# Macaron transformer on one core: GpSimd instead of SyncE writes the score terms of the later batches in the first and the last attention

## What is computed

```python
x = x + 0.5 * _L0_ffn_ref(_layernorm(x, axis=-1), ...)
x = x + _L0_attn_ref(_layernorm(x, axis=-1), ...)
x = x + 0.5 * _L0_ffn_ref(_layernorm(x, axis=-1), ...)
...
x = x + 0.5 * _L3_ffn_ref(_layernorm(x, axis=-1), ...)
x = x + _L3_attn_ref(_layernorm(x, axis=-1), ...)
x = x + 0.5 * _L3_ffn_ref(_layernorm(x, axis=-1), ...)
```

```python
qkv = (x @ qkv_w.T + qkv_b).reshape(B, T, 3, H, D)
att = jnp.einsum('bhtd,bhsd->bhts', q, k) / np.sqrt(D)
att = att + bias[None]                       # layer 0 only, and causal
att = jax.nn.softmax(att, axis=-1)
out = jnp.einsum('bhts,bhsd->bhtd', att, v)
```

## Time and profile before

| | us |
|---|---|
| median of 3 runs | 1535.95 |
| lowest and highest run | 1530.17, 1540.0 |
| the profiled execution | 1542.29 |
| its span in the trace | 1540.6 |
| first attention in the trace | about 118 to 345 |
| last attention in the trace | about 1184 to 1430 |

### The profile page before, as it was taken

The page is one execution under the profiler, slowest core; times in us unless marked ns, Lnnn a source line. Parts: engine busy times, 40 slices in busy tenths (PEclk is TensorE's granted clock), DMA queues, the critical chain, the costliest instruction groups (busy, mean ns, idle before and its releaser), DMA issues. The chain is left out here.

```text
span 1540.6 us, 30124 instructions
## 1 busy us (share of the span) xinstructions
PE 1210.5 (79%) x11545; PEld 694.1 (45%) x11553; DVE 876.5 (57%) x2261; ACT 637.1 (41%) x1318; POOL 530.9 (34%) x616
## 2 busy tenths in 40 slices
PE   3995578896978748998997976683896798898498
PEld 2663244443665524555553542432574122333277
DVE  5047467742145447778644548695137888894205
ACT  1322355551322125665562224241234376776043
POOL 5753022112320067888420001126472121212442
PEclk9997799997979968999897988685897599999699
DMA  6522422103710027665416400001433212210344
GB/s 132 154 86 82 100 78 74 51 11 84 229 57 2 0 82 203 193 183 164 145 48 75 64 7 0 0 9 47 126 112 110 72 39 68 79 30 17 85 121 121
DMA packets 147513, 128.65 MB, mean 84 GB/s; under 512 B 19101, under 2 KB 133161, under 8 KB 147376
## 3 DMA queue, kind: packets, MB, share of 16 engines
q1 hardware_dynamic: 138432, 114.08, 27.6%
q0 software_dynamic: 6304, 11.37, 2.3%
q10 hardware_dynamic: 2640, 1.36, 0.6%
HBM read 79.80 MB, written 47.69 MB: 83 GB/s over the span
## 5 line engine op out<-in xcount | busy, mean ns | idle before, releaser
L2470 DVE TENSOR_REDUCE att_maxima<-psum 128x2 f32<-128x1024 f32 (+3 forms) x384 | 355.0, 949 | 133.0 <-PE psum L2118 58.0
L2351 ACT ACTIVATE att_probs<-psum 128x512 f32<-128x512 f32 (+1 forms) x640 | 323.0, 556 | 210.5 <-PE psum L2114 86.6
L108 POOL TENSOR_TENSOR rstd<-var_eps,neg_half 128x4 f32<-128x4 f32 x44 | 45.1, 1025 | 469.4 <-DVE var_eps L99 469.4
L2097 PE MATMUL psum<-att_queries,att_keys 50*32 50x384 bf16 (+4 forms) x1280 | 156.9, 331 | 47.6 <-DMA att_queries<-att_max_t 18.5
L2103 PE MATMUL psum<-att_keys,att_queries 48*32 48x384 bf16 (+4 forms) x1280 | 154.3, 343 | 12.2 <-DVE att_maxima L2470 11.8
L1045 POOL DMA_INDIRECT returned<-moe_out,moe_slot_tokens x101 | 101.3, 1003 | 123.7 <-DVE moe_out L973 97.5
L839 ACT ACTIVATE moe_hidden<-psum,moe_b 128x320 f32<-128x320 f32 (+1 forms) x128 | 77.7, 607 | 130.3 <-PE psum L752 129.7
L2097 PEld LDWEIGHTS psum<-att_queries,att_keys 50*32 50x32 bf16 (+1 forms) x1280 | 45.8, 92 | 171.6 <-issue 91.7
L172 PE MATMUL psum<-ident,normalised_rows 128*128 128x128 f32 x192 | 43.0, 365 | 96.0 <-DVE normalised_rows L117 73.0
L759 PE MATMUL psum<-moe_w,moe_hidden 128*128 128x128 f32 (+1 forms) x784 | 109.5, 286 | 0.0
L752 PE MATMUL psum<-moe_slot_columns,moe_w 128*128 128x320 f32 (+1 forms) x256 | 101.0, 539 | 2.9 <-ACT moe_slot_columns L834 2.9
(11 more groups left out here) (296 smaller groups left out, 2339.8 us busy)
## 6 DMA issues: line engine op xcount, KB each, us to landing
score_terms<-att_parts SPq DMA_DIRECT2D x44, 384.0 KB, 2.7
moe_w<-l_w SPq DMA_DIRECT2D x64, 256.0 KB, 3.1
moe_back<-returned SPq DMA_DIRECT2D x24, 256.0 KB, 4.2
att_queries<-score_terms SPq DMA_DIRECT2D x64, 96.0 KB
att_keys<-score_terms SPq DMA_DIRECT2D x64, 96.0 KB
att_queries<-score_terms SPq DMA_DIRECT2D x16, 384.0 KB, 4.3
att_keys<-score_terms SPq DMA_DIRECT2D x16, 384.0 KB, 5.3
dispatched<-untaken SPq DMA_DIRECT2D x2, 2064.0 KB, 25.8
```

What stands on the lines that cost most here:

```text
L2097: col = nc.tensor.matmul(g.psum[one, cols_bank + h, c0:c0 + w], k_op[own_rows, ci, p, key], q_op[own_rows, ci, p, first_query[s]:T], start ...
L2351: nc.scalar.activation(probs[:, G % 2, 2 * p + r, unit_at[u]:unit_at[u] + w], g.psum[:, cols_bank + r, 0:w], ACT.Exp).then_inc(probs_ready, 1)
L2470: ins = nc.vector.tensor_reduce(maxima[:, G % 2, t, 2 * p:2 * p + 2], g.psum[:, rows_bank(k):rows_bank(k) + 2, c0:c0 + w], axis=AX, op=ALU ...
```

## The change

In the first and last attention (`split`), the writes of the terms of batches 1 to 3 are issued by GpSimd and no longer by SyncE. `write_terms(b, side)` stands right behind `low_parts(b, side)` in GpSimd's list, so side 0 is written in slot 4b-6 and side 1 in slot 4b-5 (batch 1: slots -2 and -1, where SyncE issued it in slot 0). SyncE keeps the writes of batch 0, the loads and the maxima. As two engines now issue writes, batch 0's other rows count on a semaphore of their own (`other_written`), and `await_written` picks the one to wait on. Sizes, shapes and number of transfers stay as they are.

```diff
-    def write_side(self, sp, b, side, rows, done):
+    def write_side(self, queue, b, side, rows, done):
...
-            sp.dma_start(dst[at:at + n, rows, :].rearrange("j r t -> r j t"), src).then_inc(done, 16)
+            queue.dma_start(dst[at:at + n, rows, :].rearrange("j r t -> r j t"), src).then_inc(done, 16)
...
+    def await_written(self, engine, b):
+        if b == 0:
+            engine.wait_ge(self.other_written, 16 * 6)
+        else:
+            engine.wait_ge(self.written, 16 * 6 * b)
...
         @block.sync
         def _(sp):
-            def write_terms(b):
-                if b >= 2:
-                    for i in range(RING):
-                        sp.wait_ge(op_loaded[i], 16 * op_loads * (b - 1))
-                for side in range(2):
-                    sp.wait_ge(parts_ready, 2 * b + side + 1)
-                    begun.write_side(sp, b, side, slice(0, P), written)
...
-                    sp.wait_ge(written, 16 * 6 * (b + 1))
+                    begun.await_written(sp, b)
                     begun.load_operands(sp, G)
...
-                if split and q == 0 and 1 <= b + 1 < B:
-                    write_terms(b + 1)
...
         @block.gpsimd
...
-                pool.wait_ge(written, 16 * 6 * b)
+                begun.await_written(pool, b - 1)
...
+            def write_terms(b, side):
+                if b >= 2:
+                    for i in range(RING):
+                        pool.wait_ge(op_loaded[i], 16 * op_loads * (b - 1))
+                pool.wait_ge(parts_ready, 2 * b + side + 1)
+                begun.write_side(pool, b, side, slice(0, P), begun.written)
...
                     if q in (2, 3) and 1 <= b + 2 < B:
                         low_parts(b + 2, q - 2)
+                        write_terms(b + 2, q - 2)
```

More of the change, by code:

```diff
@@ L1801, in __init__ @@
             "projected", "projections_taken", "high_parts", "remainders", "middle_parts", "parts"))
-        self.written, self.first_written = sem("terms_written"), sem("first_terms_written")
+        self.first_written, self.other_written = sem("first_terms_written"), sem("first_batch_terms_written")
+        self.written = sem("later_batches_terms_written")
         self.op_loaded = [sem(f"operands{i}") for i in range(RING)]
@@ L1894, in other_rows @@
         for side in range(2):
-            self.write_side(sp, 0, side, slice(GROUP_ROWS, P), self.written)
+            self.write_side(sp, 0, side, slice(GROUP_ROWS, P), self.other_written)
+    def await_written(self, engine, b):
[3 more added lines that the diff above has]
+            engine.wait_ge(self.written, 16 * 6 * b)
 def attention(g, name, kind, weights, gate, bias=None, routing=None, begun=None, queries=None, later=None):
@@ L1928, in attention @@
             proj, taken, hi_ready, rem_ready = begun.proj, begun.taken, begun.hi_ready, begun.rem_ready
-            mid_ready, parts_ready, written, first_written = begun.mid_ready, begun.parts_ready, begun.written, begun.first_written
+            mid_ready, parts_ready, first_written = begun.mid_ready, begun.parts_ready, begun.first_written
             ones_placed, values_zeroed, op_loaded = begun.ones_placed, begun.values_zeroed, begun.op_loaded
```

## The result

| | before | after |
|---|---|---|
| median, us | 1533.06 (4 runs) | 1518.35 (4 runs) |
| lowest and highest, us | 1529.03, 1540.0 | 1515.83, 1521.42 |
| ratio of after to before, 95% interval | | 0.9895 [0.985, 0.994] |
| the profiled execution, us | 1542.29 | 1519.0 |
| its span, us | 1540.6 | 1517.3 |

The kernel is 14.7 us faster, about 1%. A second measurement on another chip gives 0.9872 [0.9805, 0.9938]. The spans of the two profiled executions differ by 23.3 us, more than the medians do; the stages account for a part of that.

The account below looks back on a forecast made before the run. SyncE's fixed issue order, delaying group 2's maxima into ScalarE's 1290 KB transfer, was taken to bound the first attention. Terms 8.0 + 3.9 - 1.0 = 10.9 us, from 1535.95, gave 1525 us; range 1515 to 1537.

Parts of the forecast that it names:

- rival A: A direct write costs GpSimd no more than an indirect scatter: gain 15 to 17 us, time 1519 to 1521, chance 0.17.
- within 1%: Chance 0.75 that the whole kernel's time stays within about 15.4 us of before; faster 0.17, slower 0.08.
- The bound: First attention: SyncE's issue order makes group 2's maxima 8.1 us late; with ScalarE's transfer, TensorE waits 13.6 us.
- Price of a half: GpSimd's time for three writes of one side of a batch: 5.3 us, between 3.8 and 6.7.
- First boundary: Batch 1, group 2: loads of group 4 at 162.0, three maxima transfers collide, TensorE resumes 8.0 us earlier, wait 5 us.
- Second and third boundary: Groups 6 and 10 of the first attention: maxima come earlier, TensorE's waits of 2.0 and 1.9 us go, 3.9 us gained.
- Cost at groups 0 and 1: First attention: GpSimd's writes run beside the maxima of these groups, 0.5 us lost at each, -1.0 us.
- Last attention: TensorE waits there for no transfer of maxima, so earlier operands gain 0.

Follow-up runs that it names:

- before_order: Kernel before, all writes still on SyncE, with the maxima of group 4b+2 issued ahead of the loads of group 4b+4: 1576.12 us, ratio 1.0066.
- before_pieces: Kernel before with ScalarE's 1290 KB transfer in four pieces of 322 KB, one in each of slots 3 to 6: 1564.24 us, ratio 0.9997.
- before_wide: Kernel before with ScalarE's 1290 KB sent as 640 packets of 2064 bytes instead of 2560 of 516: 1554.03 us, ratio 0.9944.
- first_only: Changed kernel with GpSimd writing in the first attention only, SyncE writing in the last as before: 1522.51 us, ratio 0.986 to the kernel before.
- after_again: The changed kernel unaltered, measured again on another chip: 1530.71 us, ratio 0.9872 to the kernel before.
- after_twelve: Changed kernel with six GpSimd writes of 128 rows a half instead of three of 384, 256 and 128: 1555.12 us (1 run).
- last_only: Kernel before with GpSimd writing in the last attention only, the first left as it was: 1541.26 us, ratio 0.9987.
- after_pieces: Changed kernel with ScalarE's 1290 KB transfer in four pieces, in slots 3 to 6: 1514.69 us, ratio 0.9793; second measurement 1539.39 us, ratio 0.9826.
- after_wide: Changed kernel with ScalarE's 1290 KB sent as 640 packets of 2064 bytes instead of 2560 of 516: 1539.66 us, ratio 0.9842.
- after_slot5: Changed kernel with ScalarE's 1290 KB transfer whole but issued in slot 5 instead of slot 2: 1558.0 us, ratio 0.9943.

## Why the prediction was right, and where it was not

The time, 1518.35, lies in the range of 1515 to 1537, and the gain is 14.7 us where 10.9 was forecast. The total is closer than its terms are. By the price of a write it was rival A that came true, and a cost that no case had took back part of what A would have given. The chances leaned too far to "within 1%" (0.75): both measurements of the change lie at or past the 1% line.

**The bound.** It was read rightly. SyncE's order and the collision with ScalarE's transfer together made the 13.6 us. `before_order` attacks the order alone and loses 0.7%; of the two that attack the collision alone, `before_pieces` gains nothing and `before_wide` 0.6%. None of the three has the 1% of the earlier writes by its ratio.

**Price of a half: mis-sized.** It was taken as 5.3 us between 3.8 and 6.7. It is 2.1 to 2.2, below the lower bound. The bound took the indirect scatter as the least that a write could cost (0.97 us for 128 rows); a plain write of 128 rows costs 0.57 and one of three times the rows mostly 0.78. The text even named a possible reason, that a scatter reads indices, which no run tests, and dismissed it because a lower price gained little more. As the Trainium skill says ("DMA: Bandwidth & Descriptors", section "Anatomy of one DMA — SWDGE (gpsimd) path"), many descriptors are emitted before their incremental cost shows; these rows agree in the main, since three times the rows cost 1.4 times the issue, but at 384 rows the cost does show (0.21 us). The landing, 2.0 us behind GpSimd's end, can't be split from the issue for the last write alone; from issue to landing the median is 2.9 to 3.3 us.

**First boundary: mechanism right, 8.0 mis-sized.** With writes that end at 157.6 little of them binds. SyncE's waits in after, 154 to 176:

```profile
SPq L1884 <- PE psum L2111: 2.8, 1, 2.8
SPq L1902 <- DMA score_terms<-att_parts: 0.5, 1, 0.5
```

The loads of group 4 start when the columns of group 0 are done: 162.51 in after, where slot 0 was slow, 158.68 in `first_only` and 159.31 in `after_again`. That after has 162.5, as promised, is an accident of its clock. The maxima of group 2 are through before the 1290 KB start, 167.1 against 167.5 in `first_only`. So none of the eight collides instead of three, and the wait at group 2 is 0.8 us, not 5. That term is 13.6 - 0.8 = 12.8 us.

**The cost that was left out.** The 1290 KB did not go away. The text asked only which small transfers of the maxima they would meet, of group 2 or of group 3. What was late next was TensorE itself: 6.0, 5.7 and 5.5 us without a releaser in the three executions of kernels with the change in the first attention and the transfer as it was. Before, the same transfer ran while TensorE stood still anyway. The idle time that the old wait gave was cover for it, and the change took the cover away. `after_twelve`, where TensorE waits 5.8 us for maxima during the transfer, has no such wait.

**The sum by what was measured**, for the first attention. In `after_again` 12.9 + 3.9 - 5.5 = 11.3 us, against 12.1 found (179.7 - 167.6; `last_only`, on the same chip as `after_again`, has 180.4). In after 12.8 + 3.9 - 6.0 = 10.7, less 2.3 us for a slot 0 at half clock (10.9 us between the first exponentials of groups 0 and 1, 8.6 before) = 8.4, against 9.0 found. In `after_pieces` 12.9 + 3.9 = 16.8, and the clock that does not fall behind a wait, against 18.9 found.

**Second and third boundary, 3.9 us: right.** No wait for maxima is left at groups 6 and 10.

**Cost at groups 0 and 1, -1.0 us: not seen.** The waits for maxima there are 0.3 and 0. The slow slot 0 of after isn't this cost: `first_only` and `after_again` have the same writes at the same places and a clock of 1.00 from 156 to 165, and `before_wide`, whose writes are SyncE's, has a clock of 0.57 from 158 to 162. From 159 to 162 five of the thirteen traces have 0.50 to 0.59 (after, `after_wide`, `after_slot5`, `before_wide`, `before_pieces`) and eight 1.00. What lowers it stays open.

**Last attention, 0: right.** `last_only` is 0.9987 [0.995, 1.0024], and its last attention 193.1 us against 193.6.

**Open.** The profiled span fell by 23.3 us and the first attention by 9 to 13. The rest of the difference lies in stages whose code is the same, and which scatter by as much. That TensorE's wait is one for its own instructions is argued, and no run changes that supply; but the traces point to it. The instruction queue moves packets of 16 KB, in the first attention one about every 5 us. From one to the next TensorE runs 255 instructions in the mean, and the other engines together 23. Of after, the queues from 181 to 182:

```profile
q10 hardware_dynamic: 131, 0.06, 50.8%
q1 hardware_dynamic: 46, 0.04, 20.6%
q8 instruction: 1, 0.02, 9.0%
```

That packet starts at 181.2; the one before it had started at 170.2, ahead of the transfer and 7.8 us before TensorE stopped. In all four executions with the wait a packet starts 2.8 to 3.0 us before TensorE resumes. Where TensorE waited 4 us or more at group 2 for maxima or loads (before, `last_only`, `before_order`, `before_wide`, `before_pieces`, `after_twelve`), the next packet starts 2.7 to 4.4 us after it has resumed. So in those six the gap in the supply is an effect of the standstill, and in the four it can be the cause.

Shown is that the wait follows the transfer to slot 5, that it ends at the same distance from the transfer's issue (12.9 us in after, 12.4 in `first_only`, 12.3 in `after_again`, 12.6 in `after_slot5`), where the transfer is nearly done, and that it is gone when the same bytes go in fewer packets.

## The version that beats both

The changed kernel with the transfer cut in four (0.9793 and 0.9826) or sent in large packets (0.9842) is ahead of the changed kernel as it is (0.9872) and of the one before. The intervals of these ratios overlap, so the step from the changed kernel to these is likely and not proven by time alone; the vanished wait of 6 us is what speaks for it. Four pieces and large packets can't be told apart: 0.9826 and 0.9842 on one chip.

## What to carry to other kernels

When a change removes a long idle stretch, list the transfers that ran in that stretch, and ask what they will hold up once the engines are busy, the engines' own supply among it. Bound a price also from below with a reason, not with the nearest dearer operation. And cut a bulk fill of DRAM into large packets before looking for a better slot for it.

## What the hardware showed that was not expected

- The same 1290 KB from one queue land in 12.4 to 14.1 us as packets of 516 bytes and in 6.1 to 6.9 us as packets of 2064. As small packets they stood beside a wait of TensorE of 5.5 to 6.3 us with no releaser in the profile, in all four executions in which it did not wait for maxima or loads meanwhile; as large ones they didn't.
- A plain write issued by GpSimd mostly took 0.54 to 0.57 us for 128 rows of 1 KB and 0.78 us for 384.
- TensorE's granted clock can be 0.50 for some us in one execution and 1.00 in another of the same kernel at the same place (slot 0 of after and of `after_again`), while TensorE is busy for 3.00 of 3.00 us at the lower and 2.00 at the higher clock (159 to 162). From the first exponentials of group 0 to those of group 1 it took 10.9 us at the lower clock, against 9.1 in `after_again` and 8.6 in before.
